# Two VectorE reorderings in a fused attention and feed-forward layer: a dequantised piece's low half behind the decays, a gated product between the low halves of x

## The chip, the cores and the metric

One core of a Trainium2 chip runs the whole program. The time is the device time of one execution in microseconds, the median of three runs for the kernel before. In this text PE is TensorE, DVE is VectorE, ACT is ScalarE, POOL is GpSimd, and SP is the engine that issues the DMAs.

## The reference

The input is `x` of shape (2, 1024, 512). The layer is

```
x = x + layernorm(attention(layernorm(x)))
x = x + layernorm(ffn(layernorm(x)))
```

Attention has 32 query heads on 8 key/value heads of width 128. It adds half of a softmax attention in a sliding window (blocks of 64, rotary positions) and half of a gated linear attention, whose decay is `log_sigmoid(k) / 16`; the sum is rounded to bfloat16 and multiplied by `Wo`.

```
o_ = 0.5 * sliding_window(rope(q), rope(k), v) + 0.5 * gla_scan(softmax(q), softmax(k), v, g)
h  = silu(x @ dq1.T) * (x @ dq2.T);   ffn = h @ dq3.T
```

The three feed-forward weights are quantised and dequantised first (NF4): each block of 64 is divided by its largest magnitude, each value goes to one of 16 codes, and is multiplied back.

## The kernel before, in words

A **turn** is one key/value head of one tile of 128 tokens: 8 x 16 = 128 turns, in 32 **steps** of 4 turns. A turn has `t.i` (its step) and `t.p` (0 to 3, its place in the step). The function `turns` (L106) writes out steps 0 to 3, loops over steps 4 to 27 with a hardware loop, and writes out steps 28 to 31. Each engine has its own `turn(t)`, an order written out by hand; semaphores alone tie them. The work is pipelined over turns: in turn t an engine works on t, on `l1` (the turn before), `l2` and `l3`.

**PE, `turn` (L1442).** Projection of k and v (L1363), decays and turned k of l1 (L1308 to L1311), output projection of l3 (L1352), scores of the linear attention of l2 (L1327, L1334; they wait for `qtT` of l2), turning of q (L1318), the state product and its update (L1407, L1410; L1410 waits for `kt` of l1), turned probabilities (L1400), window scores (L1383, L1391), projection of q (L1363), turned `qe` and `kt` (L1417, L1421), output (L1428).

**DVE, `turn` (L1129).** `use_k` (L911 to L906), `q_sums` (rq, L965), in turn 1 `nf4_end` (L1070), in turn 2 `nf4_low` (L1075), then `gla_k` (kt, L945), `merge` (L985, L987; waits for PE's L1334), `add_out` (L1017), `state` (L994, L1005), `p_max` (L970; waits for PE's L1391), the decays `log_decay` and `low_decay` (L922, L923, L928), the thresholds `nf4` (L1055), `p_sums` (rp, L977), `use_q` (L933, L903, L905, L906) and `gla_q` (qtT, L955).

**The dequantisation.** There are 33 pieces of 128 x 512 weights, piece j in step j, piece 32 later. DVE makes 15 threshold images a piece in a ring of 8 (L1055: none before the next ones are free; 2, 4, 5 and 4 of them in the four turns of a step), POOL adds them one turn later (L554, `nf4_add`, 14 additions), DVE scales the sum in turn 1 of the next step (L1070, `f_dq`), ACT makes its fp16 high half in the same turn (L771, `f_w[:, 0]`), and DVE the low half, `f_dq * 256 - high` (L1075, `f_w[:, 1]`). That is `nf4_low(j)`: it waits for the high half and its semaphore `f_lod` lets SP store the piece (`store_piece`, L391). On SP, the loads of the projection weights for a later step (L337 to L341) stand behind that store.

**POOL, `turn` (L569).** `rotate_q` of l1 (qc, L520), `rotate_k` (kc, L525), `softmax_q` (qe, L531), `nf4_add` (L554), `softmax_p` (pr, L538; waits for rp), `split_low` (wl, L544).

**The feed-forward tail.** The hidden units are 11 chunks `c`; tokens are 4 groups of 4 tiles. Group 0 runs written out, `half_hidden` for gate and up (L1489), then `down(0, c - 1)` (L1507), then the next chunk. In chunks 8, 9 and 10 of group 0, four transposed tiles of the normalised x for later groups are made: PE turns one tile after each quarter of the up product (L1439, `turn_item`), ACT copies its high half (L764, `high`), DVE makes its low half (L1127, `low`). The lists are `within[c]`: four items in chunks 8 to 10, none before. DVE's `hidden` (L1214) makes `hf = up * silu(gate)`; ACT rounds it (hh, L838, behind its four high halves), POOL makes the rest (hl, L600), and `down` needs both. Turning an item waits for the low half of the item two before it, because the two share a bank. Behind `down(0, 10)` PE goes on with group 1.

The place of the first edit in DVE's turn:

```
if t.p == 2 and not (isinstance(t.i, int) and t.i == 0):
    nf4_low(t.i - 1)
```

Of the kernel before, what the change touches and what calls it, by code (L numbers as in the profile page):

```python
# [72 lines left out]
def number(t):  # L73

    return t.i * STEP + t.p if isinstance(t.i, int) else None
# [22 lines left out]
def wait_tile(eng, sem, t, back=0):  # L98

    v = t.count() - back  # L100
    if isinstance(v, int) and v <= 0:
        return
    eng.wait_ge(sem, v)
# [15 lines left out]
def layer(nc, x, wq, wk, wv, wo, wa, wb, cosc, sinc, winmask, causal, cumsum, identc, keepc, scales, dq, out):  # L119
# [6 lines left out]
    with ExitStack() as whole:  # L126
# [165 lines left out]
        within = {c: [("x", t) for t in tiles_of(c - 1)] if c > TURN_FROM else [] for c in range(FC)}  # L292
# [6 lines left out]
        def shown(item):  # L299

            j = item[1]
            tb = PW if item in early else turn_bank[where[item] % 2]
            src = [xn[:, j % STEP, c * P:(c + 1) * P] for c in range(NC)]
            return src, tb[:].rearrange("p (c n) -> p c n", c=NC), xh[:, :, j, :], xl[:, :, j, :]
# [587 lines left out]
        def _(dve):  # L892
# [15 lines left out]
            def use_k(t):  # L908
                r = t.p % 2
                wait_tile(dve, s["kv_done"], t)  # L910
                nc.vector.tensor_reduce(kmx[:, r, :], PKV[:, 0:P], AX.X, ALU.max, negate=True).then_inc(s["kmx_d"], 1)  # L911
                nc.vector.tensor_scalar(kneg, PKV[:, 0:P], 0.0, 1.0 / WSCALE, ALU.min, ALU.mult)\
                    .then_inc(s["kneg_d"], 1)
                wait_tile(dve, s["small_done"], t, 2)
                rope(t, PKV[:, 0:P], 1, kc[:, r, :], ks[:, r, :], s["krope_d"])
# [9 lines left out]
            def low_decay(t):  # L925
                r = t.p % 2
                wait_tile(dve, s["g_d"], t)
                nc.vector.tensor_tensor(gl[:, r, :], kneg, gh[:, r, :], ALU.subtract).then_inc(s["gl_d"], 1)  # L928
# [9 lines left out]
            def gla_k(t):  # L938
                r = t.p % 2
                wait_tile(dve, s["ke_ev"], t)  # L940
                nc.vector.reciprocal(rks[:, r, :], ksum[:, r, :]).then_inc(s["rks_d"], 1)
                wait_tile(dve, s["rks_d"], t)
                wait_tile(dve, s["dec_ev"], t)
                wait_tile(dve, s["u_done"], t, 2)
                nc.vector.scalar_tensor_tensor(out=kt[:, r, :], in0=ke[:, r, :], scalar=rks[:, r, :], in1=ked,  # L945
                                               op0=ALU.mult, op1=ALU.mult).then_inc(s["kt_d"], 1)
# [14 lines left out]
            def q_sums(t):  # L961
                r = t.p % 2
                wait_tile(dve, s["q_exp"], t)
                wait_tile(dve, s["qn_p"], t, 2)
                nc.vector.reciprocal(rq[:, r, :], qsum[:, r, :]).then_inc(s["rq_d"], 1)  # L965
# [42 lines left out]
            def add_out(t):  # L1008
                wait_tile(dve, s["wo_done"], t)
                a = acc[:].rearrange("p (g q) n -> p g q n", q=STEP)[:, t_index(t), t.p, :]  # L1010
                n = number(t)
                if n is not None and n < TILES - 3:

                    dve.wait_ge(s["x_norm"], n + 1)
                    nc.vector.tensor_copy(a, PW[:]).then_inc(s["acc_d"], 1)
                else:
                    nc.vector.tensor_tensor(a, PW[:], a, ALU.add).then_inc(s["acc_d"], 1)  # L1017
# [47 lines left out]
            def nf4_end(j):  # L1065
                dve.wait_ge(s["f_ad"], j * 14 + 14)
                dve.wait_ge(s["f_abs_in"], j * 80 + 80)
                if not (isinstance(j, int) and j == 0):
                    dve.wait_ge(s["f_lod"], j)
                nc.vector.scalar_tensor_tensor(out=f_dq[:], in0=f_acc[:], scalar=float(CODE[0]), in1=f_absb[:],  # L1070
                                               op0=ALU.add, op1=ALU.mult).then_inc(s["f_dqd"], 1)

            def nf4_low(j):
                dve.wait_ge(s["f_hid"], j + 1)
                nc.vector.scalar_tensor_tensor(out=f_w[:, 1, :], in0=f_dq[:], scalar=WSCALE, in1=f_w[:, 0, :],  # L1075
                                               op0=ALU.mult, op1=ALU.subtract).then_inc(s["f_lod"], 1)
# [47 lines left out]
            def low(item):  # L1124
                dve.wait_ge(r["high"], where[item] + 1)
                _, src, hi, lo = shown(item)
                nc.vector.tensor_tensor(lo, src, hi, ALU.subtract).then_inc(r["low"], 1)  # L1127

            def turn(t):  # L1129
                l1, l2, l3, n = t.back(1), t.back(2), t.back(3), number(t)  # L1130
                first = 1 if isinstance(t.i, int) and t.i == 0 else 0
                use_k(t)
                if l1.real():
                    q_sums(l1)
                if t.p == 1 and not (isinstance(t.i, int) and t.i == 0):
                    nf4_end(t.i - 1)
                if t.p == 2 and not (isinstance(t.i, int) and t.i == 0):
                    nf4_low(t.i - 1)
                if l1.real():
                    gla_k(l1)  # L1140
                if l2.real():
                    merge(l2)
                if l3.real():
                    add_out(l3)
                if l2.real():
                    state(l2)
                if l1.real():
                    p_max(l1)
                log_decay(t)
                low_decay(t)  # L1150
                if t.p > first:
                    nf4(t)
                if n == 0:
                    nf4_blocks(0)
                    nf4_rows(0)
                if t.p == 2 * first:
                    nf4_blocks(t.i + 1)
                    nf4_rows(t.i + 1)
                if x_tile_at(n):
                    x_low(x_tile_at(n), PW)  # L1160
                if item_at(n):
                    low(item_at(n))
                if n is not None and 0 <= n - LAST - 3 < STEP:
                    statistics("att", range(n - LAST - 3, n - LAST - 2))
                if n is not None and 0 <= n - LAST - 4 < STEP:
                    tile_shift("att", n - LAST - 4)
                if n is not None and 0 <= n - LAST - 6 < STEP:
                    statistics("new", range(n - LAST - 6, n - LAST - 5))
                if n is not None and 0 <= n - LAST - 7 < STEP:
                    tile_shift("new", n - LAST - 7)  # L1170
                if l1.real():
                    p_sums(l1)
                use_q(t)
                if l1.real():
                    gla_q(l1)
                if t.p == first:
                    nf4(t)
                if n in (2, 6):
                    x_statistics({2: 2, 6: 3}[n])
                if n in (0, 4, 8):  # L1180
                    x_shift({0: 1, 4: 2, 8: 3}[n])
                if n == TILES - 1:
                    dve.wait_ge(s["zeroed"], 1)
# [25 lines left out]
            def hidden(g, c):  # L1209
                n = width(c)  # L1210
                after(dve, f["sg"], FC, g, c + 1)
                after(dve, f["up"], FC, g, c + 1)
                after(dve, f["hl"], FC, g, c - 1)
                nc.vector.scalar_tensor_tensor(out=hf[0:n, c % 2, :], in0=U[0:n, :],  # L1214
                                               scalar=HSCALE / WSCALE, in1=sg[0:n, c % 2, :],
                                               op0=ALU.mult, op1=ALU.mult).then_inc(f["hf"], 1)
# [49 lines left out]
            for c in range(2, FC):  # L1266
                if c == TURN_FROM:
                    later_shift("new")
                if c == FC - 1:
                    nf4_low(32)  # L1270
                for item in within[c]:
                    low(item)
                hidden(0, c)
                if c == 2:
                    nf4_scaled(32)
                    statistics("att", later(2))
                    statistics("att", later(3))
                if c == 3:
                    later_shift("att")
                if 4 <= c <= 6:  # L1280
                    statistics("new", later(c - 3))
                if c in LATE_STEPS:
                    late_nf4(LATE_STEPS[c])
                if c == 9:
                    nf4_end(32)
# [353 lines left out]
```

## Time and profile before

| what | value |
|---|---|
| median of 3 runs | 1944.27 us (1943.83 to 1944.58) |
| the profiled execution's own time | 1944.25 us |
| its span, first to last instruction | 1942.5 us |
| PE busy | 1859.2 us, 96% |
| DVE / ACT / POOL busy | 1486.0 / 1236.8 / 1264.9 us |
| mean granted clock of PE | 0.993 |
| a weight load of SP (L337), issue to landing | 2.4 us |

Busy times are sums over the span. DVE is busy for 77% of it and is no bottleneck on average; whether PE waits for it is decided inside each turn. A step of the loop takes 47.6 us. The timeline prints each instruction's start, its duration and, in brackets, how long its engine had sat idle before it and for whom. An instruction that is issued and then held by something other than a semaphore shows a longer duration, not idle time.

### The profile page before, as it was taken

Reading aid. Unit: us, or ns where it says so; the run is one execution under the profiler, and the core shown is the slowest. Engines: PE = TensorE matmul, PEld = TensorE weight load, DVE = VectorE, ACT = ScalarE, POOL = GpSimd, SP = SyncE. Lnnn points to the kernel's source line nnn. Section 1 sums busy time; section 2 is a strip of 40 time slices with the busy share of each in tenths; the row PEclk is TensorE's granted clock in tenths of the full one; section 3 lists DMA queues with packets and bytes.
Section 4 is the critical chain, followed back from the end, with each engine's and each line's share of the span. In section 5 each row is a group of like instructions: output and inputs, shape, how many; then the busy total and the mean of one; then the engine's idle time right before and its main releaser. Section 6 shows DMA issues by size and latency. Waiting matters only on the chain.

```text
span 1942.5 us, 42961 instructions
## 1 busy us (share of the span) xinstructions
PE 1859.2 (96%) x11566; PEld 1235.4 (64%) x11566; DVE 1486.0 (77%) x3980; ACT 1236.8 (64%) x4840; POOL 1264.9 (65%) x1164
## 2 busy tenths in 40 slices
PE   4899999999999999999999999999999999999997
PEld 3667666766666666766766666766766654444443
DVE  5998888888888888888888888888899956302122
ACT  5677777777777777777777777777667645412121
POOL 2777777777777777777777777777767747212121
PEclk8999999999999999999999999999999999999999
DMA  6111111111111111111111111111201024000000
GB/s 220 55 36 43 41 45 43 43 44 44 43 43 43 42 42 42 43 47 42 42 42 42 42 42 42 42 42 42 84 30 30 23 71 147 33 0 22 0 22 22
DMA packets 85452, 90.52 MB, mean 47 GB/s; under 512 B 14216, under 2 KB 56456, under 8 KB 85384
## 3 DMA queue, kind: packets, MB, share of 16 engines
q1 hardware_dynamic: 85384, 89.71, 14.8%
q8 instruction: 31, 0.51, 0.1%
q14 instruction: 37, 0.30, 0.1%
HBM read 76.48 MB, written 13.18 MB: 46 GB/s over the span
## 4 chain that ended last, share of the span: by engine, by line
PE 62%; DVE 18%; issue 14%; POOL 4%; ACT 1%; DVEq 1%; DMA 0%; POOLq 0%; ACTq 0%
PE bank L1363 17%; PE bank L1352 8%; PE bank L1391 6%; PE bank L1334 4%; PE bank L1407 4%; PE bank L1428 4%; PE bank L1489 4%; PE bank L1400 3%; DVE f_s L1055 2%; PE bank L1318 2%; DVE f_nrm L1042 2%; PE bank L1417 2%; POOL hl L600 2%; PE bank L1507 2%; PE bank L1410 2%
## 5 line engine op out<-in xcount | busy, mean ns | idle before, releaser
L554 POOL TENSOR_TENSOR f_acc<-f_acc,f_s 128x512 f32<-128x512 f32 x429 | 547.5, 1276 | 32.6 <-POOL f_acc L554 0.4
L1363 PE MATMUL bank<-wh,xh 128*128 (+2 forms) x1024 | 334.9, 327 | 6.6 <-DVE cumh L1204 6.0
L1363 PE MATMUL bank<-wl,xh 128*128 (+2 forms) x1024 | 334.8, 327 | 0.0
L1363 PE MATMUL bank<-wh,xl 128*128 (+2 forms) x1024 | 334.6, 327 | 0.0
L538 POOL TENSOR_TENSOR pr<-pr,rp 128x512 f32<-128x512 f32 x128 | 133.2, 1041 | 241.8 <-DVE rp L977 241.5
L1055 DVE TENSOR_SCALAR f_s<-f_nrm 128x512 f32<-128x512 f32 x480 | 260.9, 603 | 3.5
L651 ACT ACTIVATE qe<-bank,nqm 128x128 f32<-128x128 f32 x512 | 180.9, 365 | 108.6 <-DVE qs L906 78.1
L1489 PE MATMUL bank<-xh,w 128*128 (+3 forms) x704 | 218.3, 379 | 1.4 <-ACT sg L832 1.4
L600 POOL TENSOR_TENSOR hl<-hf,hh 128x512 f16<-128x512 f32 (+1 forms) x44 | 51.3, 1167 | 231.9 <-ACT hh L838 231.9
L679 ACT ACTIVATE pr<-bank,pmx 128x128 f32<-128x128 f32 x512 | 180.8, 367 | 32.4 <-DVE pmx L970 24.3
L1214 DVE SCALAR_TENSOR_TENSOR hf<-bank,sg 128x512 f32<-128x512 f32 (+1 forms) x44 | 30.3, 689 | 220.5 <-PE bank L1489 205.9
L1352 PE MATMUL bank<-wh,oT 128*128 (+1 forms) x512 | 194.0, 379 | 2.6 <-DVE xl L1121 2.0
L1352 PE MATMUL bank<-wl,oT 128*128 (+1 forms) x512 | 194.0, 379 | 0.0
L520 POOL TENSOR_TENSOR qc<-qc,qs 128x512 f32<-128x512 f32 x128 | 162.4, 1269 | 23.4 <-DVE qs L906 23.4
L670 ACT ACTIVATE qrT<-bank 128x512 f32<-128x512 f32 x128 | 76.4, 597 | 132.1 <-PE bank L1318 132.1
L525 POOL TENSOR_TENSOR kc<-kc,ks 128x128 f32<-128x128 f32 x128 | 72.4, 566 | 115.7 <-DVE ks L906 115.7
L531 POOL TENSOR_TENSOR qe<-qe,rq 128x512 f32<-128x512 f32 x128 | 146.3, 1143 | 0.6 <-DVE rq L965 0.5
L1363 PEld LDWEIGHTS bank<-wh,xl 128*128 (+1 forms) x1024 | 100.5, 98 | 66.9 <-issue 0.8
L1363 PEld LDWEIGHTS bank<-wl,xh 128*128 (+1 forms) x1024 | 100.5, 98 | 66.4 <-issue 0.5
L970 DVE TENSOR_REDUCE pmx<-bank 128x4 f32<-128x512 f32 x128 | 88.2, 689 | 71.3 <-PE bank L1391 71.3
L1363 PEld LDWEIGHTS bank<-wh,xh 128*128 (+1 forms) x1024 | 100.8, 98 | 61.0 <-issue 8.2
L1391 PEld LDWEIGHTS bank<-krT,qrT 128*128 128x128 f32 x1024 | 136.2, 194 | 5.0
(178 smaller groups left out, 4975.0 us busy)
## 6 DMA issues: line engine op xcount, KB each, us to landing
f_blk<-wa SPq DMA_DIRECT2D x33, 320.0 KB, 2.9
f_raw<-wb SPq DMA_DIRECT2D x33, 256.0 KB, 2.7
dequantised<-f_w SPq DMA_DIRECT2D x33, 256.0 KB, 2.0
w<-dequantised SPq DMA_DIRECT2D x33, 256.0 KB, 4.3
raw_qkv<-wq SPq DMA_DIRECT2D x29, 256.0 KB, 2.4
raw_o<-wo SPq DMA_DIRECT2D x29, 256.0 KB, 2.6
f_recb<-scales SPq DMA_DIRECT2D x99, 64.0 KB, 2.6
f_absb<-scales SPq DMA_DIRECT2D x99, 64.0 KB, 2.6
```

What stands on the lines that cost most here:

```text
L520: nc.gpsimd.tensor_tensor(qc[:, r, :], qc[:, r, :], qs[:, r, :], ALU.add).then_inc(s["qrope_p"], 1)
L531: nc.gpsimd.tensor_tensor(v, v, rq[:, r, :].unsqueeze(2).to_broadcast([P, GRP, P]), ALU.mult).then_inc(s["qn_p"], 1)
L538: nc.gpsimd.tensor_tensor(v, v, rp[:, r, :].unsqueeze(2).to_broadcast([P, GRP, P]), ALU.mult).then_inc(s["pn_p"], 1)
L554: nc.gpsimd.tensor_tensor(f_acc[:], f_acc[:], f_s[:, step, :], ALU.add).then_inc(s["f_ad"], 1)
L600: nc.gpsimd.tensor_tensor(hl[0:n, c % 2, :], hf[0:n, c % 2, :], hh[0:n, c % 2, :], ALU.subtract)\
L651: last = nc.scalar.activation(qe[:, r, h * P:(h + 1) * P], PQ[:, h * P:(h + 1) * P], ACT.Exp, bias=nqm[:, r, h:h + 1], scale=1.0 / WSCALE, ...
L679: last = nc.scalar.activation(pr[:, r, j * P:(j + 1) * P], SC[:, j * P:(j + 1) * P], ACT.Exp, bias=pmx[:, r, j:j + 1], accum_out=psm[:, r, ...
L1055: nc.vector.tensor_scalar(f_s[:, k % 8, :], f_nrm[:], float(BOUND[k]), float(DELTA[k]), ALU.is_gt, ALU.mult).then_inc(s["f_sd"], 1)
L1352: last = nc.tensor.matmul(PW[:], oT[:, t.p % 2, h].rearrange("p b n -> p (b n)"), w[:, sl + h, QW + KVW:WW], start=(h == 0 and k == 0), st ...
L1363: last = nc.tensor.matmul(dst, av, w[:, sl + c, lo:hi], start=(n == 0), stop=(n == 3 * NC - 1))
L1391: last = nc.tensor.matmul(SC[:, j * P:(j + 1) * P], qrT[:, r, b, 2 * hp:2 * hp + 2, :].rearrange("p h n -> p (h n)"), keys, start=False, s ...
L1489: last = nc.tensor.matmul(dst[0:n, :], w12[c][:, ww, "gu".index(kind), d, 0:n], x4, start=(k == 0), stop=(k == 3 * NC - 1))
```

## The change

On DVE, `nf4_low` of the piece before moves from turn 2 of a step (ahead of `gla_k`) to turn 3 (behind the decays, ahead of the thresholds), in steps 1 to 31; and in group 0 the gated product `hidden(0, c)` stands behind two of the four low halves instead of behind all four.

```
@@ DVE turn
-                if t.p == 2 and not (isinstance(t.i, int) and t.i == 0):
-                    nf4_low(t.i - 1)
                 if l1.real():
                     gla_k(l1)
...
                 log_decay(t)
                 low_decay(t)
+                if t.p == 3 and not first:
+                    nf4_low(t.i - 1)
                 if t.p > first:
                     nf4(t)
@@ DVE, group 0
-                for item in within[c]:
+                for item in within[c][0:2]:
                     low(item)
                 hidden(0, c)
+                for item in within[c][2:]:
+                    low(item)
```

`first` is 1 in step 0 and 0 elsewhere.

## Rows read from the trace of the kernel before

**Rows 1.** The page, part 1: busy time, share, instructions.
```profile
PE 1859.2 (96%) x11566; PEld 1235.4 (64%) x11566; DVE 1486.0 (77%) x3980; ACT 1236.8 (64%) x4840; POOL 1264.9 (65%) x1164
```

**Rows 2.** The waits, PE: line <- whom: us in total, times, longest.
```profile
PE bank L1410 <- DVE kt L945: 29.2, 29, 1.7
PE bank L1327 <- DVE qtT L955: 9.2, 11, 2.1
```

**Rows 3.** Timeline of PE, step 18: start, duration, [idle before].
```profile
909.92 0.49 PE L1410 MATMUL bank<-va,kt 128*128 128x128 f32 x2 [0.97 <-DVE kt L945]
...
930.93 0.22 PE L1327 MATMUL bank<-cau,identb 128*128 128x128 bf16 x1
...
942.22 0.38 PE L1352 MATMUL bank<-wl,oT 128*128 x1
942.51 0.23 PE L1327 MATMUL bank<-cau,identb 128*128 128x128 bf16 x1
```

**Rows 4.** Timeline of DVE, turn 2 of step 18.
```profile
918.78 0.81 DVE L1075 SCALAR_TENSOR_TENSOR f_w<-f_dq,f_w 128x512 f16<-128x512 f32 x1
...
920.69 0.29 DVE L985 SCALAR_TENSOR_TENSOR pr<-bank,pr 128x128 f32<-128x128 f32 x1 [0.63 <-PE bank L1334]
...
929.24 0.68 DVE L955 TENSOR_TENSOR qtT<-bank,edT 128x512 f32<-128x512 f32 x1
```

**Rows 5.** Timeline of DVE, the first threshold of turn 2.
```profile
925.09 0.96 DVE L1055 TENSOR_SCALAR f_s<-f_nrm 128x512 f32<-128x512 f32 x1
```

**Rows 6.** Timeline of DVE, turn 3 of step 18.
```profile
936.59 1.26 DVE L1055 TENSOR_SCALAR f_s<-f_nrm 128x512 f32<-128x512 f32 x1
937.77 1.49 DVE L1055 TENSOR_SCALAR f_s<-f_nrm 128x512 f32<-128x512 f32 x1
...
939.18 0.75 DVE L1055 TENSOR_SCALAR f_s<-f_nrm 128x512 f32<-128x512 f32 x2
...
941.78 0.68 DVE L955 TENSOR_TENSOR qtT<-bank,edT 128x512 f32<-128x512 f32 x1
```

**Rows 7.** Timeline of POOL, turns 2 and 3 of step 18.
```profile
918.59 0.45 POOL L525 TENSOR_TENSOR kc<-kc,ks 128x128 f32<-128x128 f32 x1 [0.25 <-DVE ks L906]
919.01 1.49 POOL L531 TENSOR_TENSOR qe<-qe,rq 128x512 f32<-128x512 f32 x1
...
924.50 1.26 POOL L554 TENSOR_TENSOR f_acc<-f_acc,f_s 128x512 f32<-128x512 f32 x1
...
931.26 1.04 POOL L531 TENSOR_TENSOR qe<-qe,rq 128x512 f32<-128x512 f32 x1
...
936.30 1.26 POOL L554 TENSOR_TENSOR f_acc<-f_acc,f_s 128x512 f32<-128x512 f32 x1
...
937.64 1.33 POOL L554 TENSOR_TENSOR f_acc<-f_acc,f_s 128x512 f32<-128x512 f32 x1
```

**Rows 8.** Timeline, SP's weight load in step 18 and ACT's use of one.
```profile
929.39 0.33 SPq L337 DMA_DIRECT2D raw_qkv<-wq  x1
```
```profile
901.37 0.43 ACT L706 ACTIVATE raw_qkv<-raw_qkv 128x256 f32<-128x256 f32 x1
```

**Rows 9.** Timeline of DVE, the thresholds of turn 3 in step 3.
```profile
220.71 3.59 DVE L1055 TENSOR_SCALAR f_s<-f_nrm 128x512 f32<-128x512 f32 x4
```

**Rows 10.** Timeline, chunk 10 of group 0: PE, ACT, DVE, POOL.
```profile
1665.65 0.38 PE L1489 MATMUL bank<-xh,w 128*96 128x512 f16 x1
...
1670.36 0.61 PE L1507 MATMUL bank<-w,hh 96*128 96x512 f16 x2 [1.31 <-POOL hl L600]
```
```profile
1666.50 0.60 ACT L764 ACTIVATE xh<-bank 128x512 f16<-128x512 f32 x1 [0.49 <-PE bank L1439]
1668.45 0.63 ACT L838 ACTIVATE hh<-hf 96x512 f16<-96x512 f32 x1 [1.35 <-DVE hf L1214]
```
```profile
1667.74 0.68 DVE L1214 SCALAR_TENSOR_TENSOR hf<-bank,sg 96x512 f32<-96x512 f32 x1
```
```profile
1669.16 1.15 POOL L600 TENSOR_TENSOR hl<-hf,hh 96x512 f16<-96x512 f32 x1 [8.36 <-ACT hh L838]
```

More of the change, by code:

```diff
@@ L1136, in turn @@
                     nf4_end(t.i - 1)
-                if t.p == 2 and not (isinstance(t.i, int) and t.i == 0):
-                    nf4_low(t.i - 1)
                 if l1.real():
@@ L1150, in turn @@
                 low_decay(t)
+                if t.p == 3 and not first:
+                    nf4_low(t.i - 1)
                 if t.p > first:
@@ L1270, in _ @@
                     nf4_low(32)
-                for item in within[c]:
+                for item in within[c][0:2]:
                     low(item)
                 hidden(0, c)
+                for item in within[c][2:]:
+                    low(item)
                 if c == 2:
```

## The prediction

> **What bounds the kernel now.** I read the page's busy times first: PE is busy for 96% of the span [rows 1], so the kernel is faster or slower only by PE's own idle time. Then the waits of PE [rows 2]: it waited 29 times for `kt`, 29.2 us in all, and 11 times for `qtT`, 9.2 us. Both come from DVE, the engine that the change reorders. Then the timeline of one step of the loop, because a total does not say in which turn a wait falls. The wait of 0.97 us for `kt` is in turn 1 [rows 3]. The moved instruction stands ahead of `kt` in turn 2, one turn later, and there DVE afterwards sits idle 0.63 us for PE's L1334 [rows 4]: in turn 2 DVE is early and PE sets the pace. At the end of turn 2 it is early too: `qtT` ends at 929.24 + 0.68 = 929.92 and PE takes it at 930.93, 1.0 us later [rows 3, 4].
>
> Turn 3 is the other way round. `qtT` ends at 941.78 + 0.68 = 942.46 [rows 6]. PE's matmuls of 512 columns follow each other at 0.22 us, so after the one at 942.22 the next could start at 942.44; it starts at 942.51, 0.05 us after `qtT` [rows 3]. It is too short a wait to be printed, but the slack is gone: whatever is put ahead of `qtT` in turn 3 goes to PE in full. The move takes 0.81 us from a turn with 1.0 us to spare and puts it where there is nothing.
>
> **What the lock does.** The printed durations say that DVE and POOL hold each other up. Two undisturbed thresholds take 0.75 together: 0.42 for the last, and 0.34 from one to the next, since they overlap a little [rows 6]. The one at 936.59 takes 1.26 and ends at 937.85, 0.29 after POOL's addition, which ends at 936.30 + 1.26 = 937.56. The one at 937.77 takes 1.49 and ends at 939.26, 0.29 after POOL's next addition at 937.64 + 1.33 = 938.97 [rows 6, 7]. So a threshold that meets a POOL operation waits for its end and then needs 0.29. The moved instruction obeys this as well: issued at 918.78 it ends at 919.59, 0.55 after POOL's `kc` at 918.59 + 0.45 = 919.04 [rows 4, 7]. And it holds POOL: `qe`, issued at 919.01, takes 1.49 where one turn later it takes 1.04 [rows 7]. It ends at 920.50, 0.91 after the DVE instruction's end, so POOL starts some 0.13 before that end is recorded. An addition of 1.26 held in this way ends 1.13 after DVE.
>
> The Trainium skill, page "SBUF — State Buffer", section "Who interferes with whom", has this as an exclusive lock on a port pair that the two share, taken by the first to issue "for the whole instruction". By its word an instruction let in after a wait would still need its whole recorded time. The rows say less (0.29 for a threshold of 0.42, 0.55 for the low half), and I take the rows. By the page alone the low half and the threshold behind it would each need some 0.13 more (0.42 - 0.29, taken for both), 0.26 a step.
>
> **Part A, the move, per step of the loop.** What goes in turn 2: the low half, and with it POOL's hold-up. POOL's `qe` is 1.49 - 1.04 = 0.45 shorter, so its four additions of turn 2 end 0.45 earlier. The last of them (924.50 + 1.26 = 925.76) held up DVE's first threshold (925.09 + 0.96 = 926.05, again 0.29 behind) [rows 5, 7], so the thresholds, rp, the rotations and `rq` of DVE all come 0.45 earlier as well. POOL's chain waits for them (`qc`, `kc`, `qe`), so its five additions of turn 3 start 0.45 earlier. PE gains nothing by it: it was not waiting here. The decays of turn 3 still come when PE's window scores let them, so DVE's place in turn 3, 936.59, stays.
>
> What is added in turn 3, worked out on that clock: POOL's fourth addition ends at 937.56 - 0.45 = 937.11. The low half, issued at 936.59, ends 0.55 later, at 937.66. POOL's fifth addition, asked for meanwhile, ends 1.13 after that, 938.79. The first threshold ends 0.29 later, 939.08, and three more at 0.34 each make 940.10. Before, it was 939.18 + 0.75 = 939.93 [rows 6]. The difference of 0.17 is a sum of eight rounded numbers; I take 0.15. So 0.81 us of instruction costs 0.15 us a step: the thresholds had stood waiting for POOL anyway, and POOL is ahead by what it had been held up. For the 24 steps of the loop, 4 to 27, that is 24 x 0.15 = +3.6 us, all on PE's path by way of L1327. What is queued behind the low half (thresholds, rp, use_q, `qtT`, and POOL's `softmax_p` behind rp) comes 0.15 later, and PE with it. The wait for `kt` of 0.97 in the next turn 1 stays, since both sides of it move alike.
>
> Bounds for a step: without the 0.45 from POOL the same sum ends at 940.54, +0.6. If the low half fell wholly into time that DVE loses to POOL anyway, 0. The worst is its whole undivided 0.81. I take 0.15, the value that the rows give directly.
>
> **The seven steps outside the loop** (1 to 3, 28 to 31) have POOL's additions in other places. In step 3 the first threshold slips in ahead of one, and the four take 3.59 [rows 9]. The same working gives about +0.2, +0.5, +0.4 for steps 1 to 3 and +0.3, +0.1, +0.1, +0.5 for 28 to 31, net of what two of them regain in turn 2, where PE does wait (the two `qtT` and `kt` waits there are among those of [rows 2]). Sum +2.0; bounds 0 and 7 x 0.81 = 5.7. It is nearer to the lower end because each keeps POOL's 0.45.
>
> **What else the moved instruction sets.** It now waits for ACT's high half a turn longer after it was made: no wait. `f_lod` comes some 18 us later, and SP's store with it. SP's weight loads stand behind the store: issued at 929.39 now [rows 8], about 938.3 afterwards. ACT first needs them in the next turn 0, at 901.37 + 47.6 = 949.0 [rows 8]; with three issues and the 2.4 us to landing, some 7 us are left. The price is 0; without that cover it would be one late weight piece a step. The scale of the next piece needs `f_lod` a turn and a half later: 0.
>
> **Part B, the gated product.** Chunks 8 and 9 have no wait of PE behind them, because the down product and the gate product of the next chunk lie between. Chunk 10 has: PE sits 1.31 us for POOL's `hl` [rows 10]. The chain now: fourth high half 1666.50 + 0.60 = 1667.10, fourth low half, gated product at 1667.74, hh at 1668.45, hl at 1669.16 to 1670.31, PE at 1670.36. Afterwards the product needs only the up product's end, 1665.65 + 0.38 = 1666.03, and runs 1666.1 to 1666.8, beside the fourth high half. ACT makes hh behind that, 1667.1 to 1667.7; POOL makes hl 1667.8 to 1668.95; PE starts at 1669.0. That is 1.4 us earlier: PE's previous product would let it start at about 1668.9, so the wait is nearly gone and its neighbour, PE's own order, is next. The third and fourth low halves end by about 1668, before DVE's next work. Bounds 0 and -1.4; I take -1.4, since every duration is a row.
>
> **Sum.** 3.6 + 2.0 - 1.4 = +4.2 against the profiled execution's own 1944.25 (span 1942.5 and 1.75 around it): 1948.4. The median 1944.27 is the same within 0.02. A measurement of this kernel can tell about 0.2%, 3.9 us, from no change, so the forecast lies just at that edge.
>
> **The rivals.**
> - **Absorbed, and not slower.** The one mechanism: POOL's lead in turn 3. The 0.15 is 0.60 less the lead; from a lead of 0.60 the addition costs nothing, and above it gains. For it: POOL waits for DVE at several places (`kc` waited 0.25 [rows 7]), each of which could pass on more than 0.45. Against: nothing in the rows gives a second 0.15. With a cost of 0 in the loop and 0.7 outside: 1943.5; with a lead of 0.7, 1941. Chance 0.22, a third of it faster by over 0.2%.
> - **The `kt` wait shrinks.** If the 29 waits of 0.97 were of the turn with the low half, 29 x 0.81 = 23.5 us would go, 1921. Against: the turn, as read above. Chance 0.05.
> - **POOL's 0.45 does not arrive in turn 3**, because ACT or PE times DVE's rotations there. 24 x 0.6 = 14.4 and 4 outside: 1961. Against: `qtT` of turn 2 has 1.0 us of slack and no wait for PE stands between. Chance 0.08.
> - **The low half is let in later** than the rows of a short wait say: it waits 0.5 us here and waited 0.3 there. With up to 0.13 more a step (a threshold's 0.42 less 0.29), 24 x 0.13 = 3.1: 1951.5. Against: the two held thresholds waited 1.0 and 1.2 us and both needed 0.29. Chance 0.08.
>
> **How the numbers follow.** The forecast has the remaining 0.57, with its own range 1946.3 to 1950.5; slightly more than half of it (0.30) lies above 1948.2. Slower by over 0.2%: 0.30 + 0.08 + 0.08 = 0.46. Within: 0.27 + 0.15 = 0.42. Faster: 0.07 + 0.05 = 0.12. The range takes in the absorbed case and the later low half, and leaves out 1921 and 1961: 1942 to 1953.
>
> **What would show it.** In turn 3 of the loop the low half takes about 1.07 (936.59 to 937.66), the sum of the four thresholds shrinks to about 2.5, `qtT` ends 0.15 later against the decays, and PE's wait at L1327 in turn 0 grows to about 0.2. The `kt` wait of turn 1 stays 0.97. In turn 2 POOL's `qe` takes 1.04 and DVE's idle time at L985 grows to about 1.4. A step takes 47.75. At the end of group 0 PE's wait for `hl` is at most 0.1. I am wrong if the step is 47.6 or less, or if the `kt` wait has changed.

## The result and the profile after

The changed kernel takes 1952.03 us, the median of 7 runs (1948.05 to 1953.07), beside 1944.38 us for the kernel before (1943.83 to 1946.04, 7 runs). The ratio is 1.0032, with a 95% interval of 1.0021 to 1.0043: slower, by 0.3%. The forecast was 1948.4, in a range of 1942 to 1953. The execution that was profiled is the shortest of the seven, 1948.05 with a span of 1946.2, and it matches the forecast; the median lies 3.6 us above the forecast, and many of the experiments below ask why.

Line numbers of PE are 2 higher in the changed kernel: L1410 is L1412, L1327 is L1329. The waits of PE in the changed kernel, which answer to [rows 2]:

```profile
PE bank L1412 <- DVE kt L945: 28.6, 29, 1.7
PE bank L1329 <- DVE qtT L955: 10.7, 12, 2.5
```

Neither row seems to hold 4 us. The wait for `kt` is what it was, and the printed waits for `qtT` grew by 1.5. The rest is spread over the loop in pieces too short to be printed. They show in the timeline of PE in the changed kernel, step 18, which answers to [rows 3]:

```profile
912.78 0.49 PE L1412 MATMUL bank<-va,kt 128*128 128x128 f32 x2 [0.96 <-DVE kt L945]
...
945.07 0.38 PE L1354 MATMUL bank<-wl,oT 128*128 x1
945.54 0.23 PE L1329 MATMUL bank<-cau,identb 128*128 128x128 bf16 x1
...
960.54 0.38 PE L1412 MATMUL bank<-va,kt 128*128 128x128 f32 x1 [0.96 <-DVE kt L945]
```

From the matmul at 945.07 PE could have gone on at 945.29. It starts 0.25 later, where it was 0.07 in [rows 3], so this wait grew by 0.18. The two waits for `kt` lie one step apart: 47.76 us. Over the 22 steps from the `kt` wait of step 5 to that of step 27 the changed kernel takes 1050.6 us (292.02 to 1342.60), the one before 1047.5 (290.94 to 1338.41): 0.14 more a step.

DVE and POOL in turn 3 of step 18 in the changed kernel, which answer to [rows 6] and the last of [rows 7]:

```profile
939.44 1.09 DVE L1075 SCALAR_TENSOR_TENSOR f_w<-f_dq,f_w 128x512 f16<-128x512 f32 x1
940.45 2.51 DVE L1055 TENSOR_SCALAR f_s<-f_nrm 128x512 f32<-128x512 f32 x4
...
944.81 0.67 DVE L955 TENSOR_TENSOR qtT<-bank,edT 128x512 f32<-128x512 f32 x1
```
```profile
938.71 1.27 POOL L554 TENSOR_TENSOR f_acc<-f_acc,f_s 128x512 f32<-128x512 f32 x1
940.06 1.61 POOL L554 TENSOR_TENSOR f_acc<-f_acc,f_s 128x512 f32<-128x512 f32 x1
```

The low half takes 1.09, because it waits for POOL's fourth addition, which ends at 939.98; the low half ends at 940.53, 0.55 later. The fifth addition is held in turn and takes 1.61 instead of 1.33; and the four thresholds take 2.51 instead of 3.35 (936.59 to 939.93 in [rows 6]). From the issue of the low half to the end of the last threshold is 3.52 us (939.44 to 942.96), against 3.35 for the thresholds alone before.

DVE and POOL in turn 2 of step 18 in the changed kernel, which answer to [rows 4, 5, 7]:

```profile
923.55 0.29 DVE L985 SCALAR_TENSOR_TENSOR pr<-bank,pr 128x128 f32<-128x128 f32 x1 [1.02 <-PE bank L1336]
...
927.95 1.86 DVE L1055 TENSOR_SCALAR f_s<-f_nrm 128x512 f32<-128x512 f32 x5
```
```profile
921.86 1.04 POOL L531 TENSOR_TENSOR qe<-qe,rq 128x512 f32<-128x512 f32 x1
```

POOL's `qe` takes 1.04 instead of 1.49 and the five thresholds 1.86 instead of 2.31, which stood so in the kernel before: the lead of 0.45.

```profile
925.09 2.31 DVE L1055 TENSOR_SCALAR f_s<-f_nrm 128x512 f32<-128x512 f32 x5
```

At the end of group 0 in the changed kernel (DVE, ACT, POOL, PE), which answers to [rows 10]:

```profile
1671.41 0.69 DVE L1214 SCALAR_TENSOR_TENSOR hf<-bank,sg 96x512 f32<-96x512 f32 x1 [0.47 <-PE bank L1491]
```
```profile
1672.29 0.62 ACT L838 ACTIVATE hh<-hf 96x512 f16<-96x512 f32 x1
```
```profile
1672.98 1.15 POOL L600 TENSOR_TENSOR hl<-hf,hh 96x512 f16<-96x512 f32 x1 [8.35 <-ACT hh L838]
```

The gated product now waits for PE's up product alone and runs beside ACT's last high half. `hl` ends at 1674.13, and no wait of PE for it is left among its waits.

### The profile page after: what moved, and what is told of

It reads as the page before. It is cut to its first block, busy times and chain, and to the rows that moved or that the text cites. A ratio compares the mean times of both kernels' runs of the same rounds, so it can differ in the third digit from the quotient of the medians.

```text
span 1946.2 us, 42833 instructions
## 1 busy us (share of the span) xinstructions
PE 1854.4 (95%) x11438; PEld 1235.4 (63%) x11566; DVE 1458.1 (75%) x3980; ACT 1236.4 (64%) x4840; POOL 1259.0 (65%) x1164
## 4 chain that ended last, share of the span: by engine, by line
PE 54%; DVE 21%; issue 18%; POOL 4%; DVEq 1%; ACT 1%; DMA 0%; POOLq 0%; ACTq 0%
PE bank L1365 13%; PE bank L1393 7%; PE bank L1354 6%; PE bank L1336 4%; PE bank L1409 4%; PE bank L1491 4%; DVE f_s L1055 4%; PE bank L1402 3%; PE bank L1430 3%; PE bank L1320 2%; DVE qtT L955 2%; PE bank L1509 2%; DVE f_nrm L1042 2%; PE bank L1412 2%; POOL hl L600 2%
## 5 line engine op out<-in xcount | busy, mean ns | idle before, releaser
L554 POOL TENSOR_TENSOR f_acc<-f_acc,f_s 128x512 f32<-128x512 f32 x429 | 555.7, 1295 | 33.0 <-DVE f_s L1062 0.8
L1055 DVE TENSOR_SCALAR f_s<-f_nrm 128x512 f32<-128x512 f32 x480 | 221.1, 520 | 3.5
L1354 PE MATMUL bank<-wh,oT 128*128 (+1 forms) x512 | 194.1, 379 | 3.7 <-DVE xl L1121 2.7
L1354 PE MATMUL bank<-wl,oT 128*128 (+1 forms) x512 | 194.1, 379 | 0.0
L1393 PE MATMUL bank<-krT,qrT 128*128 128x128 f32 x1024 | 136.7, 277 | 7.8 <-ACT qrT L670 1.2
```

Source lines behind the costliest of these rows:

```text
L554: nc.gpsimd.tensor_tensor(f_acc[:], f_acc[:], f_s[:, step, :], ALU.add).then_inc(s["f_ad"], 1)
L1055: nc.vector.tensor_scalar(f_s[:, k % 8, :], f_nrm[:], float(BOUND[k]), float(DELTA[k]), ALU.is_gt, ALU.mult).then_inc(s["f_sd"], 1)
L1354: last = nc.tensor.matmul(PW[:], oT[:, t.p % 2, h].rearrange("p b n -> p (b n)"), w[:, sl + h, QW + KVW:WW], start=(h == 0 and k == 0), st ...
L1393: last = nc.tensor.matmul(SC[:, j * P:(j + 1) * P], qrT[:, r, b, 2 * hp:2 * hp + 2, :].rearrange("p h n -> p (h n)"), keys, start=False, s ...
```

## The experiments

Two theories stood at the start, each with a rival. The **lock theory** is the forecast's: the low half waits for POOL and holds POOL, the thresholds lose less time behind it, and POOL's lead from turn 2 pays most of it. Its rival is that only the turn counts. **Theory A** is for the 3.6 us of the median: other executions have one more stretch of PE at 1.2 GHz, the lower of its two levels. Its rival: they have other waits at the full clock. **A1** and **A2**, which come later, say where in the program that stretch arises. In the edits below `...` stands for lines that are not shown.

### The changed kernel once more

No edit.

> The changed kernel once more. Its profiled execution took 1948.05 us, which is the 1944.25 of before plus what the steps of the forecast add (+3.8), but its other executions took up to 1953.07, the median 1952.03. The granted clock listed with them is 0.995 for 1948.05 and 0.992 or 0.993 for 1952 to 1953. Theory A: those executions have one more stretch of some 6.8 us at half clock, at a place where PE works (a stretch costs half its length, 3.4 us). Rival: they have longer waits at a full clock, a DVE and POOL meeting that falls otherwise. Under A a profile of such an execution shows a step of the loop of 47.76 us as the first one, and one more half-clock stretch. Under the rival it shows another step length.

Measured: 1951.71 us (1949.34 to 1952.24, 8 runs), ratio 1.0029 (1.0018 to 1.0039) to 1945.61 us (25 runs of the kernel before, 1943.30 to 1946.67). The profiled execution took 1952.04, so this time a long one was caught. Its step in the loop is 47.76 us (294.29 to 1344.93 over 22 steps), that of the short one. So for this execution theory A holds in kind and its rival falls. The size was wrong: it is not one more stretch of 6.8 us but three short ones, of which the windows of seven us around 92, 232 and 1478 us show a granted clock of 0.76. The 4.0 us by which its span exceeds the short one's can be laid out: it is 0.35 late at the first `kt` wait (48.52 against 48.17), another 1.9 at the wait of step 5 (294.29 against 292.02), 0.1 more by the long wait of step 29, 1.5 behind it, and 0.1 in the tail.

A third batch of the changed kernel gives the clearest pair:

> The changed kernel on the same chip and beside the one with step 29 put back, for that comparison: median 1951.7 to 1952.1, as twice before.

Measured: 1951.81 us (1949.41 to 1952.42, 7 runs), ratio 1.0034 (1.0022 to 1.0045). Its profiled execution took 1949.41. Here is the table by stretches (us, busy time and count of PE, PEld, DVE, ACT, POOL, granted clock, DMA share, GB/s), first the short execution of 1948.05, then this one:

```profile
1469.00:1476.00 7.00, 4.49 (x35) 3.02 (x34) 6.93 (x20) 2.13 (x10) 4.59 (x5) 1.00 0.09 34
1476.00:1483.00 7.00, 6.95 (x43) 4.98 (x44) 5.52 (x18) 6.50 (x29) 6.57 (x7) 1.00 0.00 0
```
```profile
1469.00:1476.00 7.00, 4.49 (x35) 3.05 (x34) 6.76 (x22) 2.51 (x13) 4.74 (x5) 1.00 0.03 13
1476.00:1483.00 7.00, 6.93 (x32) 4.68 (x33) 4.21 (x13) 5.06 (x23) 6.39 (x6) 0.76 0.00 0
```

Up to 1476 PE's part is the same. PE was busy for 4.49 of the 7 us before, since it had waited 2.51 us for `qtT`. Then the granted clock is 1.00 in one and 0.76 in the other: part of the stretch ran at 1.2 GHz. The timelines show what that does to an instruction, PE in the short execution and in this one:

```profile
1475.24 0.23 PE L1329 MATMUL bank<-cau,identb 128*128 128x128 bf16 x1 [2.51 <-DVE qtT L955]
...
1476.87 1.02 PE L1409 MATMUL bank<-qtT,sr 128*128 128x512 f32 x2
...
1490.62 0.49 PE L1412 MATMUL bank<-va,kt 128*128 128x128 f32 x2 [1.22 <-DVE kt L945]
```
```profile
1474.86 0.23 PE L1329 MATMUL bank<-cau,identb 128*128 128x128 bf16 x1 [2.51 <-DVE qtT L955]
...
1476.64 1.91 PE L1409 MATMUL bank<-qtT,sr 128*128 128x512 f32 x2
...
1491.92 0.38 PE L1412 MATMUL bank<-va,kt 128*128 128x128 f32 x1 [1.23 <-DVE kt L945]
```

The same two matmuls take 1.02 and 1.91, and from the `qtT` wait to the next `kt` wait it is 15.38 us in one and 17.06 in the other. Such a stretch costs 1.7 us here. The profile of 1952.04 us has the same one (1477.62 to 1494.54, 16.92 us), beside the two in the first eighth of the program.

### The move alone, and the product alone

The move without the product's edit, and the product's edit without the move:

```
+                if t.p == 3 and not first:          (first kernel only)
+                    nf4_low(t.i - 1)
+                for item in within[c][0:2]: ...     (second kernel only)
```

> Part A alone: the low half in turn 3 of steps 1 to 31, the gated product behind all four low halves. By the forecast +5.3 us on the 1944.25 of before (24 x 0.146 in the loop, +2 outside) at an undisturbed clock: 1949.6, and 1.4 above the changed kernel. If the gated product were what brings the slow executions, this kernel would have none and stay at 1949.6 in all of them; if the move does, it has them too, at about 1953.5.

> Part B alone: the gated product between the low halves in group 0, the low half of the piece left in turn 2. By the forecast -1.4 us: 1942.8 to 1943.0. PE's wait for hl at the end of group 0 goes from 1.31 to under 0.1; no step of the loop changes (47.61). If it is the move that brings the slow executions, all times of this kernel lie within 1 us, but for the half-microsecond scatter of before.

Measured: the move alone 1951.99 us (6 runs, 1950.05 to 1953.84), ratio 1.0036 (1.0024 to 1.0048). The product alone 1943.83 us (11 runs, 1942.40 to 1945.09), ratio 0.9992 (0.9983 to 1.0001); its step is 47.60. The move makes the kernel slower, and the product's edit gives back about 1 to 1.8 us, which its interval just fails to tell from nothing; the wait for `hl` of 1.31 is gone in its trace and is there in the other's. The expectation that the move alone would be 1.4 us above the changed kernel did not come in by medians: 1951.99 is 0.3 above 1951.71, from six and eight executions that spread over 3 to 4 us. The traces do show it: from PE's last wait for `qtT` to the end of the span the move alone takes 373.9 us (1575.39 to 1949.3) and the changed kernel 372.4 (1573.78 to 1946.2), which is 1.5 less. The profile of the move alone has a stretch at 1.2 GHz at the place just shown, so the product's edit does not bring it. My expectation that all times of the product alone would lie within 1 us was wrong: they spread over 2.7 us, as those of before do over 3.4. A stretch at 1.2 GHz near 92 us is in this profile, in that of 1952.04 us and in that of the low half early in turn 3 below (granted clock 0.76 from 91 to 98), and not in the changed kernel's short one (1.00).

### The move in the loop alone

```
+                if t.p == 2 and isinstance(t.i, int) and t.i != 0:   (steps 1-3, 28-31)
+                    nf4_low(t.i - 1)
...
+                if t.p == 3 and not isinstance(t.i, int):            (steps 4-27)
+                    nf4_low(t.i - 1)
```

> The changed kernel with the move in the loop's steps 4 to 27 alone; steps 1 to 3 and 28 to 31 keep the low half in turn 2. By the forecast 24 x 0.146 - 1.4 = +2.1 against before: 1946.4. Theory A1: the extra half-clock stretch belongs to steps 28 to 31, where PE's waits for qtT grew to 1.49, 2.51 and 1.53 us; then this kernel has none and all its executions lie near 1946.4. Rival A2: it belongs to the start of the program or to the loop; then this kernel has slow executions at about 1950 as well.

Measured: 1947.65 us (11 runs, 1945.87 to 1948.83), ratio 1.0011 (1.0002 to 1.0020); step 47.75. The loop's 24 moves with the product's edit cost 2.0 us against before (1945.61), where the sum had 2.1. The 1946.4 expected was counted from the one profiled execution of before, and the median is 1.2 above it as the median of before is 1.4 above that execution. The seven steps outside the loop, which the sum put at +2.0, make the other 4.1 of the changed kernel's 1951.71. None of its eleven runs reaches 1949, and its profile has no stretch at 1.2 GHz between 68 and 1937 us. This is for theory A1.

### Step 29 moved alone, and step 29 alone put back

```
-                if t.p == 2 and not (isinstance(t.i, int) and t.i == 0):
+                if t.p == 2 and not (isinstance(t.i, int) and t.i in (0, 29)):
...
+                if t.p == 3 and isinstance(t.i, int) and t.i == 29:
+                    nf4_low(t.i - 1)
```

> The kernel before with the low half moved to turn 3 in step 29 alone. At full clock the move there is worth about +0.1 us (POOL's lead gives back in turn 2 what the low half costs in turn 3); PE's wait for qtT at the end of step 29 grows from 1.92 to about 2.5 us. Theory A1 (this longer wait is what sends the clock to 1.2 GHz behind it, as in the two profiles with a stretch at 1477): a 3.4 us stretch at half clock near 1472, +1.6 to +2 us in most executions, median about 1947. Rival: the stretch comes with the move in all steps together; then the median stays within 0.5 us of the kernel before.

Measured: 1946.24 us (10 runs, 1945.11 to 1948.92), ratio 1.0008 (0.9998 to 1.0017). The profile has what A1 asks for: the wait of 2.51 us, and a lower clock behind it (PE in this kernel; then two rows by stretches):

```profile
1470.06 0.29 PE L1329 MATMUL bank<-cau,identb 128*128 128x128 bf16 x1 [2.51 <-DVE qtT L955]
```
```profile
1462.00:1469.00 7.00, 5.56 (x38) 3.70 (x36) 6.93 (x15) 2.56 (x10) 4.45 (x5) 1.00 0.10 37
1469.00:1476.00 7.00, 5.88 (x32) 5.27 (x34) 4.45 (x17) 4.74 (x24) 6.71 (x7) 0.76 0.00 0
```

But the median moved by 1.0 us only, between A1's 1.8 and the rival's 0.5, and the interval includes no change. The times do not decide; the trace does for one execution. There the stretch cost 1.4 us: from the `kt` wait at 1432.99 to the one at 1486.83 it is 53.8 us, where the kernel before takes 52.4 (1433.54 to 1485.93). The reverse, the changed kernel with step 29 in turn 2:

```
-                if t.p == 3 and not first:
+                if t.p == 3 and not first and not (isinstance(t.i, int) and t.i == 29):
...
+                if t.p == 2 and isinstance(t.i, int) and t.i == 29:
+                    nf4_low(t.i - 1)
```

> The changed kernel with step 29 alone put back (its low half in turn 2). At full clock this is worth nothing (within 0.2 us). Theory A1: PE's wait for qtT at the end of step 29 is 1.9 us again instead of 2.5, no half-clock stretch follows it near 1477, and the executions lie mostly at 1948 to 1950.5, median some 1.5 us under the changed kernel's. Rival: the stretch is the sum of the longer waits of steps 28 to 31; then it stays, and the median is 1951.7 to 1952.

Measured: 1950.94 us (7 runs, 1948.68 to 1951.71), ratio 1.0032 (1.0021 to 1.0044), beside the changed kernel's 1951.81 on the same chip: 0.9 less, where A1 said 1.5 and its rival about nothing. The trace has what neither foresaw. The stretch at 1.2 GHz behind 1477 is gone, but there is one 14 us earlier (PE in this kernel, then rows by stretches):

```profile
1461.73 0.23 PE L1331 MATMUL bank<-cau,identb 128*128 128x128 bf16 x1 [2.12 <-DVE qtT L955]
...
1475.78 0.23 PE L1331 MATMUL bank<-cau,identb 128*128 128x128 bf16 x1 [0.66 <-DVE qtT L955]
```
```profile
1455.00:1462.00 7.00, 4.88 (x37) 3.34 (x35) 6.86 (x20) 2.25 (x9) 3.44 (x4) 1.00 0.00 0
1462.00:1469.00 7.00, 6.95 (x36) 5.08 (x36) 4.13 (x16) 5.45 (x26) 6.57 (x7) 0.76 0.01 2
```

It follows PE's wait of 2.12 us, one turn ahead of the other. And it is nearly free: PE is slower there, and its next wait for `qtT` is 0.66 instead of the 1.92 of the kernel before. From the `kt` wait at 1438.43 to the one at 1491.18 it is 52.7 us, 0.4 more than before. So A1 as it was put, with no stretch behind a shorter wait, is wrong, but the cost went with the wait of 2.51, and the times cannot tell the two theories apart.

The twelve profiles can be counted for steps 28 to 30. Six have a wait for `qtT` of 2.5 us, and five of them a lower clock behind it: all but the changed kernel's short one. Six have one of 2.0 to 2.1, and two of them a lower clock behind it: this kernel and the scaled sum below. Four have one of 1.9 and none has a lower clock there; behind one of 1.77 in the doubled kernel below there is one. So a long wait makes the drop likelier and does not ensure it. Two of these waits, PE in the doubled kernel and in that of the scaled sum (the granted clock is 0.76 from 1492 to 1499 in the one and from 1441 to 1448 in the other):

```profile
1493.70 0.23 PE L1333 MATMUL bank<-cau,identb 128*128 128x128 bf16 x1 [2.51 <-DVE qtT L955]
```
```profile
1441.54 0.29 PE L1329 MATMUL bank<-cau,identb 128*128 128x128 bf16 x1 [2.04 <-DVE qtT L955]
```

### The low half made twice

```
+                if t.p == 2 and not first:
+                    nf4_low(t.i - 1, False)      (no semaphore; the one in turn 3 counts)
```

> The changed kernel, with the low half made twice: in turn 2 ahead of gla_k, as before, and again in turn 3 (the same values). Theory (POOL's lead pays): with the first one back in turn 2, POOL comes 0.45 later to turn 3, the low half and the thresholds there end 0.45 later, and each step of the loop costs 0.45 more than the changed kernel's 47.76: 48.2, in all 24 x 0.45 = +10.8, about +12 with the steps outside: 1960 at an undisturbed clock, 1962 to 1965 with the half-clock stretches. Rival (the low half is cheap in turn 3 only because the thresholds wait for POOL anyway, whatever turn 2 does): the added one lies in DVE's idle time of turn 2, and the step stays at 47.76, the time at 1952.

Measured: 1966.44 us (4 runs, 1965.92 to 1968.78), ratio 1.0108 (1.0091 to 1.0125). The step is 48.33 us, 0.57 more than the changed kernel's, where 0.45 and a time of 1960 to 1965 were expected. DVE in turn 3 of this kernel:

```profile
949.82 1.54 DVE L1075 SCALAR_TENSOR_TENSOR f_w<-f_dq,f_w 128x512 f16<-128x512 f32 x1
951.29 2.50 DVE L1055 TENSOR_SCALAR f_s<-f_nrm 128x512 f32<-128x512 f32 x4
```

Made in turn 2, where DVE has idle time enough to hide it, the instruction still costs 0.45 us a turn later: the low half of turn 3 takes 1.54 instead of 1.09, the thresholds what they took. The other 0.12 is PE's wait for `kt`, 1.08 instead of 0.96. The rival that whatever happens in turn 2 is free falls. Without that 0.12 the step is 0.60 above the 47.61 of before, which is the price that the forecast set for a move without POOL's lead.

### The low half early in turn 3

```
-                if t.p == 2 and not (isinstance(t.i, int) and t.i == 0):
+                if t.p == 3 and not (isinstance(t.i, int) and t.i == 0):
                     nf4_low(t.i - 1)
                 if l1.real():
                     gla_k(l1)
```

> The changed kernel with the low half in turn 3 but ahead of gla_k, not behind the decays. DVE has idle time behind that place in turn 3 (for PE's L1336 and L1393), so its own 0.8 us cost nothing; but it now meets POOL there, and POOL's lead of 0.45 from turn 2 is lost again before the thresholds. Theory: the thresholds of turn 3 run as in the kernel before, the step is 47.61, the time that of the gated product alone, 1942.4 to 1943.8. Rival (the turn alone counts): 47.76 and 1950 to 1952.

Measured: 1944.23 us (10 runs, 1942.31 to 1945.56), ratio 0.9992 (0.9983 to 1.0002), step 47.59. DVE in turn 3 of this kernel:

```profile
932.79 0.81 DVE L1075 SCALAR_TENSOR_TENSOR f_w<-f_dq,f_w 128x512 f16<-128x512 f32 x1
...
938.81 3.34 DVE L1055 TENSOR_SCALAR f_s<-f_nrm 128x512 f32<-128x512 f32 x4
```

These lines are against the kernel before; the gated product is as changed. The same turn costs nothing when the instruction stands in front of DVE's idle time. It takes its old 0.81, POOL's lead is gone, and the thresholds take their old 3.34. The rival that the turn alone counts falls: 0.15 us a step belong to the place behind the decays. (The expected time, 1942.4 to 1943.8, was missed by 0.4; the kernel with the product's edit alone took 1943.83.)

### The other instruction: the scaled sum behind add_out

```
-                if t.p == 1 and not (isinstance(t.i, int) and t.i == 0):
-                    nf4_end(t.i - 1)
                 ...
                 if l3.real():
                     add_out(l3)
+                if t.p == 1 and not (isinstance(t.i, int) and t.i == 0):
+                    nf4_end(t.i - 1)
```

These lines are against the kernel before. The low half is in turn 2, the gated product as changed.

> The low half back in turn 2, the gated product as in the changed kernel, and the other DVE instruction of the dequantisation moved: nf4_end (f_dq, L1070) from ahead of gla_k in turn 1 to behind add_out in turn 1. There PE waits 0.97 us for kt in every step, and f_dq stands 0.58 ahead of kt. Expected: kt 0.58 earlier, the wait 0.39, a step 47.0; 29 steps x 0.58 = 17 us less than the gated product alone: 1926 to 1928. Rival: POOL, whose kc and qe are no longer held up, meets f_dq behind add_out, and the window maximum and the decays come later, so that another wait takes its place; then half of it or less, 1935.

Measured: 1926.81 us (4 runs, 1924.46 to 1927.15), ratio 0.9901 (0.9885 to 0.9918), the fastest of all, faster than both kernels, and inside the expected 1926 to 1928. The waits of PE in this kernel, and DVE around the moved instruction:

```profile
PE bank L1412 <- DVE kt L945: 13.4, 29, 1.7
...
PE bank L1329 <- DVE qtT L955: 7.1, 9, 2.0
```
```profile
900.57 0.35 DVE L945 SCALAR_TENSOR_TENSOR kt<-ke,rks,bank 128x128 f32<-128x128 f32 x1
...
901.96 0.68 DVE L1070 SCALAR_TENSOR_TENSOR f_dq<-f_acc,f_absb 128x512 f32<-128x512 f32 x1
```

The wait for `kt` is 0.36 in a step instead of 0.97, 13.4 us in all instead of 29.2, and a step takes 47.01. The rival, that another wait would take the place of this one, falls. The waits that the forecast read by turn show turn 2 off PE's path; they show turn 1 on it, and there the same kind of move pays.

## Why the prediction was right, and what it left out

**The number.** The median lies in the range, but 3.6 us above the forecast and outside the band of 1946.3 to 1950.5 that the forecast gave its own mechanism. The range reached to 1953 for the sake of rivals, and the one nearest to the measured time, a later low half at 1951.5, is not what happened. That 1952.03 fell inside is in part luck: a cost that the sum does not have, of the clock, lies in it.

**The turn.** Right. In the loop no wait of PE ended in turn 2, and the wait for `kt` stayed at 0.96.

**0.15 us a step.** Right. The step grew by 0.14 to 47.76. Its parts came as summed: the low half 1.09 for 1.07, the thresholds 2.51 for about 2.5, L1329's wait 0.25 for about 0.2, POOL's `qe` 1.04 for 1.04. DVE's idle time at L985 is 1.02 and not the 1.4 forecast: that engine also waits 0.40 ahead of `kt` now (the low half had covered it), and PE does not notice.

**How long the lock is held.** The low half waited longer here (0.5 us) than in the row it was priced from (0.3) and needed as little afterwards. The rival with 0.13 more a step falls, and with it the forecast's literal reading of the Trainium skill, page "SBUF — State Buffer", section "Who interferes with whom": by a whole recorded duration behind every wait the step would have grown by 0.4. The page's main sentence, that the second to issue blocks fully, fits the rows above: the low half ends 0.55 us after the addition ahead of it, and the addition behind it 1.14 after the low half.

**POOL's lead.** Right, and shown by taking it away: +0.45 in the doubled kernel, and the old thresholds in the early one.

**The gated product.** Forecast -1.4 with `hl` 1.31 to nearly 0. The wait is gone. In the times it is -1.8 by medians (1943.83 against 1945.61), -0.9 by the lowest (1942.40 against 1943.30), and -1.5 in the traces, as shown above.

**The seven steps outside the loop.** The forecast's terms add up to 2.1, not 2.0. The waits grew where the sum had them: for `qtT` 0.42 to 0.54, 0.16 to 0.55, 1.17 to 1.49 and 1.06 to 1.53 behind steps 2, 3, 28 and 31 (the timelines of PE), against +0.5, +0.4, +0.3 and +0.5. Three of the places went otherwise: step 1 cost nothing (PE stands at its wait at 130.31 in both kernels) where 0.2 was forecast, behind step 2 part of it stands at L1354 (0.18, for `xl`), and behind step 29 the wait moved from one turn to the next, 2.12 and 1.92 becoming 1.57 and 2.51, as netted. By PE's last wait for `qtT` the changed kernel is 5.3 us behind (1573.78 against 1568.48), where the sum has 5.6, and the spans differ by 3.8.

**The store and the weight loads.** Right. SP issues the load of step 18 at 941.33; the step stands 2.9 us later than before by then (939.44 against 936.59 in [rows 6]), so that is 938.5 against the 938.3 forecast, and ACT has no wait for these pieces in the loop.

**What was left out.** The forecast has no term for the clock. Where the clock adds nothing the change costs what it said: the profiled execution took 1948.05 (+3.8 on the profiled one before, +4.75 on the lowest of 25 runs of before). The profile before has one more stretch at 1.2 GHz near 22 us, but it costs nothing: both kernels reach their first `kt` wait at the same time (48.20 and 48.17). But only 1 of the 22 runs of the changed kernel in three batches was that short; the others lie at 1949.3 to 1950.3 (8 runs) and 1951.7 to 1953.1 (13). Of its three profiles the two of 1949.41 and 1952.04 have a stretch at 1.2 GHz behind the wait of 2.51 us in step 29, worth 1.5 to 1.7 us; the one of 1948.05 has none. The loop-only kernel, whose waits there are the old ones, costs what its sum says. In the largest batch the times of both kernels fall into two groups about 2 us apart: before at 1943.3 to 1944.0 (8 runs) and 1945.1 to 1946.7 (17), changed at 1949.3 to 1950.1 (3) and 1951.7 to 1952.2 (5). From group to like group it is 6.6 and 5.9 us by medians, which is the forecast's 4.2 and 1.7 to 2.4 more. So of the median's surplus over the forecast, 2 to 3.6 us depending on the batch of before, 1.5 to 1.7 are put down to this stretch. In the batches with the larger surplus the median of before lies in the lower group and that of the changed kernel in the upper, and the step between the groups is the rest. In the profile of 1952.04 that step is the two early stretches (1.9 us). That it is the same in the other executions is inferred from their times and not shown.

**What stays open.** Why the clock falls behind one wait of 1.8 or 2.1 us and not behind another of 2.5; whether steps 28, 30 and 31 add to it; and how often the stretch of step 29 comes. Behind 2.5 us it was seen in five profiles of single executions and missing in one, which is few, and neither the kernel with step 29 alone nor the one without it moved the median as far as A1 said.

## What to carry to other kernels

Count the waits of an engine by turn before an instruction is moved: the one that looks loaded on average may be idle in the turn in question and full in the next. The same low half cost nothing early in turn 3 and 0.15 us a step behind the decays, and an instruction of its size taken out of the way of `kt` in turn 1 gained 0.6 us a step. Where VectorE and GpSimd hold each other up, price a move by the ends of both engines' instructions and carry the other engine's lead or lag into the next turn. Where a change lengthens TensorE's longest waits, allow for a stretch at its lower clock behind them, which costs less where the next wait takes it up (0.4 against 1.7 us), and compare several executions before a difference of 0.2% is explained.

## What the runs showed of the hardware that was not expected

- A VectorE instruction with two SBUF operands that is held by GpSimd needs 0.55 us after the other's end whether it had waited 0.3 us (0.81 in all), 0.5 (1.09) or 1.0 us (1.54); undisturbed it takes 0.66 to 0.69.
- An instruction hidden in idle time of its own engine (the low half in turn 2 of the doubled kernel) cost 0.45 us a step through GpSimd, one turn later: the low half of turn 3 took 1.54 instead of 1.09.
- TensorE fell to 1.2 GHz at a wait of 2.5 us in the profiles of five executions (the changed kernel twice, the move alone, step 29 alone, the doubled low half) and of 2.0 to 2.1 us in two (step 29 put back, the scaled sum later), and stayed at 2.4 GHz after 2.51 us in the changed kernel's shortest. The two matmuls of L1409 took 1.91 instead of 1.02, and the whole cost was 1.7 us.
- The same stretch one turn earlier, ahead of another wait for VectorE, cost 0.4 us, because that wait shrank from 1.92 to 0.66.
